# Recurrent mixing and mixture-of-experts layer: another order for the first two turns, 32-byte list entries, logits kept in place, and waits of the scattered adds moved to SyncE

## The reference, cut to what matters

```python
x = x + wkv(w, u, layernorm(x), ctx)        # 16 sequences of 128 tokens, 512 channels
h = layernorm(x)
router = softmax(h @ gate_w.T)              # 8 experts, the best 2 of each token
moe = sum over the 2 of prob * (silu(h @ g_e.T) * (h @ u_e.T)) @ d_e.T      # 256 wide
sh = (silu(h @ sg.T) * (h @ su.T)) @ sd.T   # shared expert, 1024 wide
out = x + moe + sigmoid(h @ seg.T) * sh
```

## Time and profile before

| what | us |
|---|---|
| median of three runs | 589.91 |
| lowest and highest of them | 588.55, 594.93 |
| the profiled execution's own time | 594.29 |
| its span in the trace | 592.4 |
| PE busy in the span | 499.7 (84%) |
| DVE, POOL, ACT busy | 424.5, 334.8, 276.9 |

### The profile page before, as it was taken

The page is one execution under the profiler, slowest core; times in us unless marked ns, Lnnn a source line. Parts: engine busy times, 40 slices in busy tenths (PEclk is TensorE's granted clock), DMA queues, the critical chain, the costliest instruction groups (busy, mean ns, idle before and its releaser), DMA issues.

```text
span 592.4 us, 10167 instructions
## 1 busy us (share of the span) xinstructions
PE 499.7 (84%) x2703; PEld 266.4 (45%) x2703; DVE 424.5 (72%) x986; ACT 276.9 (47%) x534; POOL 334.8 (57%) x421
## 2 busy tenths in 40 slices
PE   1025899899989999999999976899999999999950
PEld 1012355455545555555554543455545555555520
DVE  4398896989888899898998875366656556555530
ACT  4639847484754765847645431333323233323210
POOL 5185956848657478486684450425364655555342
PEclk9999889999989999999999989799999999999995
DMA  8941105224544142132110400315566666766552
GB/s 313 394 172 32 37 18 178 37 71 143 45 82 161 38 148 83 55 143 72 55 35 24 143 18 20 91 35 105 97 109 104 116 108 108 132 111 115 92 71 36
DMA packets 25896, 58.42 MB, mean 99 GB/s; under 512 B 6308, under 2 KB 6450, under 8 KB 24306
## 3 DMA queue, kind: packets, MB, share of 16 engines
q0 software_dynamic: 9792, 20.65, 20.2%
q1 hardware_dynamic: 16050, 37.13, 19.7%
HBM read 37.69 MB, written 20.08 MB: 98 GB/s over the span
## 4 chain that ended last, share of the span: by engine, by line
PE 37%; DMA 17%; issue 13%; DVE 11%; POOL 7%; ACT 7%; POOLq 6%; SPq 1%; DVEq 0%; ACTq 0%
PE GU L878 21%; DMA out<-wall,idsa 11%; PE DN L893 10%; POOLq L575 5%; DMA xb<-x 4%; ACT wall L700 2%; PE HT L823 2%; PE XT L823 2%; DVE st L1076 2%; DMA out<-xb 1%; DVE wall L1066 1%; POOL out L579 1%; DVE hb L1192 1%; DVE th L1189 1%; POOL lists L469 1%
## 5 line engine op out<-in xcount | busy, mean ns | idle before, releaser
L878 PE MATMUL GU<-wall,xt 128*128 128x512 f16 x768 | 192.2, 392 | 4.4 <-DVE wall L1170 4.4
L893 PE MATMUL DN<-wall,hx 128*128 128x512 f16 (+1 forms) x618 | 153.1, 384 | 9.0 <-DVE hx L1197 5.2
L878 PEld LDWEIGHTS GU<-wall,xt 128*128 128x128 f16 x768 | 76.9, 102 | 75.9 <-issue 10.9
L579 POOL DMA_INDIRECT out<-wall,idsa x39 | 61.8, 1585 | 81.5 <-issue 41.5
L893 PEld LDWEIGHTS DN<-wall,hx 128*128 128x128 f16 x618 | 60.4, 99 | 85.3 <-DVE hx L1197 9.4
L657 ACT ACTIVATE hx<-HT 128x256 f16<-128x256 f32 x103 | 39.1, 380 | 125.8 <-PE HT L823 119.7
L1197 DVE TENSOR_TENSOR hx<-HT,hx 128x256 f16<-128x256 f32 x103 | 43.1, 419 | 64.8 <-ACT hx L657 49.5
L652 ACT ACTIVATE th<-GU,scl 128x256 f32<-128x256 f32 x103 | 48.6, 472 | 82.9 <-PE GU L878 80.0
L878 PE MATMUL GU<-wall,kb 128*128 x240 | 61.4, 379 | 0.2 <-DVE kb L1371 0.2
L1189 DVE SCALAR_TENSOR_TENSOR th<-th,GU 128x256 f32<-128x256 f32 x103 | 41.6, 404 | 24.7 <-ACT th L652 21.9
L878 PE MATMUL GU<-wall,xnb 128*128 x228 | 58.5, 379 | 0.2 <-DVE xnb L1371 0.2
(11 more groups left out here) (164 smaller groups left out, 756.4 us busy)
## 6 DMA issues: line engine op xcount, KB each, us to landing
wall<-wgu SPq DMA_DIRECT2D x12, 1024.0 KB, 9.0
wall<-wd SPq DMA_DIRECT2D x12, 512.0 KB, 10.6
xb<-x SPq DMA_DIRECT2D x16, 256.0 KB
cb<-ctx_t SPq DMA_DIRECT2D x16, 256.0 KB
xn_rows<-xnb SPq DMA_DIRECT2D x16, 256.0 KB
out<-xb SPq DMA_DIRECT2D x16, 256.0 KB
out<-yb SPq DMA_DIRECT2D x4, 256.0 KB
xb<-xn_rows,idsi POOLq DMA_INDIRECT x39
```

The lines of the kernel that those rows point to most:

```text
L579: pool.indirect_dma_start(out, bass.IndirectOffsetOnAxis(ap=idsa[:, j:j + 1], axis=0), ye[j % RESULTS], None, compute_op=ALU.add).then_inc ...
L878: ins = nc.tensor.matmul(GU[par][:], lhs(xp, c), gate_up(base, wp, c), start=m == 0, stop=m == 3 * HC - 1)
L893: ins = nc.tensor.matmul(DN[:], hx[par][:, hp * IE + c * P:hp * IE + (c + 1) * P], down(base, wp, c), start=start and m == 0, stop=stop an ...
```

## The change

Seven edits, made together:

1. The lists for tiles 0 and 1 have another order on POOL, ACT, PE and DVE. `keys(0)` goes ahead of the decay terms. The statistics of tile 2 go behind `add_now(1)`. On ACT the squares of a unit are cut in two (`gu_square`, `d_square`) and the exponentials and `second_norm(0)` come between them.
2. Zeros and padding numbers come from the row buffers 3, 4 and 5 of `xb`, not from `yb` and `xnb`. The waits of `quotient(0)` and `second_norm(0)` go, and `load_x(3)` gets one. `load_x(2)` is issued ahead of the eight DMAs.
3. An entry of a list has 32 bytes (LW = 8 int32), so a scatter writes 32 bytes a token and the initial DMA and the gather of the lists move eight times the bytes. `ids_back` lies in the growth and decay buffers, and the copy L1404 takes every eighth element.
4. The logits are written to their final place by ACT, and the maximum by DVE; two copies (L1140, L1141) go, and TOP_STEPS falls from 5 to 3.
5. The waits of the adds stand on SP. SP loads the four numbers, waits, and raises `may_add`; POOL waits for that alone.
6. `shared_gu_lo(1)` stands ahead of the turns instead of in turn 2.
7. `first_stats` waits for the former statistics to have been taken.

```diff
-TOP_STEPS, GATE_STEPS, NORM_STEPS, SCALE_STEPS = 5, 1, 3, 10
+LW = 8
+TOP_STEPS, GATE_STEPS, NORM_STEPS, SCALE_STEPS = 3, 1, 3, 10
...
-        ids_dram = nc.dram_tensor("lists", ((LISTS + 1) * P, 1), I32).ap()
+        ids_dram = nc.dram_tensor("lists", ((LISTS + 1) * P, LW), I32).ap()
...
+        zeros, pad_rows = xb[:, 3 * XW:3 * XW + H], xb[:, 4 * XW:4 * XW + P * LW]
...
             def load_x(t):
+                if t == 3:
+                    sp.wait_ge(ids_zst, ZEROS * 16)
...
+            load_x(2)
             sp.wait_ge(ids_zero, 2)
-            sp.dma_start(xn_dram[PADS:PADS + P, 0:H], yb[:]).then_inc(ids_zst, 16)
+            sp.dma_start(xn_dram[PADS:PADS + P, 0:H], zeros).then_inc(ids_zst, 16)
...
-            load_x(2)
-            sp.dma_start(ids_tiles[0:LISTS, :], xnb[:, 0:P].bitcast(I32)).then_inc(ids_zst, 16)
+            sp.dma_start(ids_tiles[0:LISTS, :], pad_rows.bitcast(I32)).then_inc(ids_zst, 16)
...
+            sp.wait_ge(waits_rdy, WAIT_STEPS)
+            for j in range(1, NSLOT):
+                for r in range(min(j, RESULTS)):
+                    if j < RESULTS:
+                        sp.wait_ge(added[r], 16)
+                    else:
+                        earlier = sp.value_load(before_i[0:1, r * NSLOT + j:r * NSLOT + j + 1],
+                                                min_val=16, max_val=16 * ((NSLOT + RESULTS - 1) // RESULTS))
+                        sp.wait_ge(added[r], earlier)
+                        plain(sp, earlier)
+                sp.sem_inc(may_add, 1)
...
             def quotient(t):
-                if t == 0:
-                    pool.wait_ge(ids_zst, ZEROS * 16)
...
             other_consts()
+            first_product(0)
             norm(1, 0, agg1, norm1, k_rdy)
-            first_product(0)
             second_product(0)
-            pool.wait_ge(nd, 1)
-            norm(2, 0, agg1, norm1, k_rdy)
+            scales(0, ROUTER)
+            nc.gpsimd.tensor_scalar(scale(ROUTER, YINV), scale(ROUTER, TANH), 2.0, None,
+                                    ALU.mult).then_inc(scale_step, 1)
+            quotient(0)
             first_product(1)
             second_product(1)
-            quotient(0)
-            scales(0, ROUTER)
-            nc.gpsimd.tensor_scalar(scale(ROUTER, YINV), scale(ROUTER, TANH), 2.0, None,
-                                    ALU.mult).then_inc(scale_step, 1)
-            pool.wait_ge(nd, 2)
             norm(0, 1, agg2, norm2, xn_rdy)
             scales(1, SHARED)
+            norm(2, 0, agg1, norm1, k_rdy)
+            quotient(1)
             norm(3, 0, agg1, norm1, k_rdy)
-            quotient(1)
             first_product(2)
             second_product(2)
...
                 if j == 0:
                     pool.wait_ge(out_st, 16 * B)
-                if j == RESULTS:
-                    pool.wait_ge(waits_rdy, WAIT_STEPS)
-                for r in range(min(j, RESULTS)):
-                    if j < RESULTS:
-                        pool.wait_ge(added[r], 16)
-                    else:
-                        earlier = pool.value_load(before_i[0:1, r * NSLOT + j:r * NSLOT + j + 1],
-                                                  min_val=16, max_val=16 * ((NSLOT + RESULTS - 1) // RESULTS))
-                        pool.wait_ge(added[r], earlier)
-                        plain(pool, earlier)
+                wait_from(pool, may_add, j)
...
             first_norm(0)
             both_exps(0)
-            shared_square(0)
+            gu_square(0)
             first_norm(1)
-            shared_square(1)
+            d_square(0)
+            gu_square(1)
             both_exps(1)
-            shared_square(2)
-            first_norm(2)
-            shared_square(3)
+            d_square(1)
...
+            gu_square(2)
+            d_square(2)
+            gu_square(3)
             second_norm(0)
+            d_square(3)
             act_hi(0)
             shared_gu_hi(0)
+            first_norm(2)
             shared_gu_hi(1)
...
             keys_t(1)
+            y_back(0)
+            xn_t_(0)
+            sum_squares(1, 2 * SU + 1, 0)
             pe.wait_ge(consts, CONSTS)
             keys_t(2)
-            y_back(0)
-            sum_squares(1, 2 * SU + 1, 0)
-            xn_t_(0)
             y_back(1)
...
+            keys(0)
...
-            keys(0)
             first_stats(1)
             small_steps(k=0)
-            keys(1)
             scan_e(0)
             scan_ev(0)
             add_now(0)
-            first_stats(2)
+            keys(1)
             reciprocals(0, 0, HC)
+            residual_and_stats(0)
             scan_e(1)
             scan_ev(1)
+            small_steps(k=1)
             add_now(1)
-            residual_and_stats(0)
-            small_steps(k=1)
-            first_stats(3)
-            reciprocals(1, 0, HC)
-            keys(2)
+            first_stats(2)
...
             act_lo(0)
+            reciprocals(1, 0, HC)
             shared_gu_lo(0)
+            first_stats(3)
+            keys(2)
+            shared_gu_lo(1)
...
-                if t is not None:
-                    TS(span(lga, t * E, E), lgt[:, 0:E], 1.0, None, ALU.mult).then_inc(top, 1)
-                    TS(span(mxa, t, 1), mx8[:, 0:1], 1.0, None, ALU.mult).then_inc(top, 1)
```

More of the change, by code:

```diff
@@ L137, in build @@
         kb, yb, xnb = sb("kb", [P, H]), sb("yb", [P, H]), sb("xnb", [P, H])
-        growth, decay = sb("growth", [P, HC * T]), sb("decay", [P, HC * T])
+        by_time = sb("by_time", [P, 2 * HC * T])
+        growth, decay = by_time[:, 0:HC * T], by_time[:, HC * T:2 * HC * T]
         th = [sb(f"th{i}", [P, IE]) for i in range(2)]
@@ L382, in other_consts @@
                 assert link.n == CONSTS
-                pool.memset(yb[:], 0.0).then_inc(ids_zero, 1)
-                pool.iota(xnb[:, 0:P].bitcast(I32), [[1, P]], base=PADS, channel_multiplier=0).then_inc(ids_zero, 1)
+                pool.memset(zeros, 0.0).then_inc(ids_zero, 1)
+                pool.iota(pad_rows.bitcast(I32), [[1, P], [0, LW]], base=PADS, channel_multiplier=0).then_inc(ids_zero, 1)
             def norm(t, k, stats_rdy, steps, used):
@@ L614, in second_norm @@
                 wait_from(act, xn_st, 16 * t)
-                if isinstance(t, int) and t == 0:
-                    act.wait_ge(ids_zst, ZEROS * 16)
                 nc.scalar.activation(xnb[:], xrow(t), ACT.Identity, bias=nrm[:, 1, 3:4],
@@ L1304, in logits_off_max @@
                 step(TT(r_d[:, first * E:last * E].rearrange("p (t e) -> p t e", e=E),
-                        lga[:, first * E:last * E].rearrange("p (t e) -> p t e", e=E),
-                        mxa[:, first:last].unsqueeze(2).to_broadcast([P, n, E]), ALU.subtract))
+                        lga[:, first * RN:last * RN].rearrange("p (t e) -> p t e", e=RN)[:, :, 0:E],
+                        mxa[:, first * 8:last * 8].rearrange("p (t e) -> p t e", e=8)[:, :, 0:1].to_broadcast([P, n, E]),
+                        ALU.subtract))
             def probabilities(k, first, last):
```

49 lines of the change are left out of this document (24 added, 25 removed).

## The result

The changed kernel takes 571.84 us (median of 4 runs, 571.03 to 573.75) against 591.96 us for the kernel before in the same comparison (4 runs, 588.55 to 594.93). The ratio is 0.9666, with a 95% interval of 0.9600 to 0.9733: some 20 us faster. The forecast was 566.0, with a range of 556 to 577. So the sign and the range held, and the gain was put some 6 us too high. The profiled execution took 573.75 us, the longest of the four, with a span of 570.1.

What follows compares the result with a forecast made beforehand. The prediction took PE to bound the middle (busy 84% of the span), with gains where it idles or runs slow. Terms 9 + 6.1 + 3.8 + 0 + 4.6 + 4.4 = 27.9 took 594.29 to 566.4; it said 566, range 556 to 577.

Steps and rivals of the forecast that it cites:

- start: First tiles, up to PE's start on the shared units: waits for tile 2's x and the zeros go, 9 us (4 to 12).
- store and load near 160, and passage: 32-byte entries quicken the store and load near 160 (3.8 us) and the passage from turns to slots (6.1 us).
- logits: Turns: two small DVE copies go, gaining 0 (0 to 5), since `chosen` is held in place of L1140.
- slots and tail: Adds with their waits on SP: 4.6 us in the slots (3 to 6), 4.4 at the end (2 to 6).
- the 45 that it had named as a sign of being wrong: Start: the prediction called itself wrong if PE starts on the shared units later than 45 us.
- the reciprocals run about 18 to 21.3: Start, DVE: the reciprocals run there instead of 29.27 to 32.6, 11 us earlier.
- to 29.3; PE's sum and DVE's exponents end near 31, POOL's scales (3 us) near 34: Start: ACT's last weight square ends at 29.3, so ACT makes the first high half at 34 instead of 44.03.
- 34.4 + 3.35 + 2.33 = 40.1 for PE's start: Start: with DVE's `reciprocals(1)` ahead of the low half, PE starts at 40.1 against 49.65.
- The lower end, from the 1664 rows: Scatters of 32 bytes: as quick as the probabilities' 1664 rows of 32 bytes, under 2 ns a row against 31.
- the 3.8 us near 160: Gap and slow products around the slow store and load near 160: 3.8 us gained, perhaps only in the profiled execution.
- no-stall rival: Near 339: `chosen` is not held, or the shifted order misses POOL's subtractions; 561 us, chance 0.12.
- slower rival: Adds: SP's waits exceed PE's 4.58 us a slot, so adds and gathers fall behind; 597 us, chance 0.02.

Runs made afterwards that it cites:

- e2: Changed kernel with list entries still 32 bytes apart, but a scatter writing only the first 4 bytes of each: 571.24 us, ratio 0.9618.
- e3: Changed kernel with the loads and waits of the adds back on POOL instead of SP: 579.99 us, ratio 0.9755.
- f3: Changed kernel with every number of the adds loaded and waited for twice on SP: 624.04 us, ratio 1.0541.
- e4: Changed kernel with entries of 4 bytes and the adds' loads and waits back on POOL: 588.77 us, ratio 0.9909.
- e1: Changed kernel with list entries of 4 bytes again (LW = 1): 581.08 us, ratio 0.9792.
- e5: Changed kernel with POOL's fill of zeros and padding numbers moved behind `second_product(0)`: 571.56 us, ratio 0.9655.
- e6: Changed kernel with the last square of the shared weights ahead of `second_norm(0)` on ACT and its sum ahead of `xn_t_(0)` on PE: 568.09 us, ratio 0.9602.
- e8: Changed kernel with the edits of e5, e6 and e7 together, and `y_back(1)` behind the first unit on PE: 569.17 us, ratio 0.9603.
- e7: Changed kernel with `first_product(2)` ahead of `norm(3, 0)` on POOL: 571.36 us, ratio 0.9664.
- f1: Changed kernel with list entries 16 bytes apart, of which a scatter writes 4 bytes: 568.51 us, one execution.
- f4: Changed kernel with the edits of e6 and e7, and ACT's `shared_gu_hi(3)` moved from ahead of the turns into turn 2: 567.95 us, ratio 0.9599.
- f2: Changed kernel with list entries 8 bytes apart, of which a scatter writes 4 bytes: 572.58 us, one execution.

## Why the prediction was right, and where it was wrong

The sum of the prediction beside the profiled executions:

| term | predicted | by the trace | by the runs |
|---|---|---|---|
| start | 9 (4 to 12) | 3.4 at the store of tile 2 (4.9 to 5.2 in e2, e3, f3) | 3.8 (e4 to before; 3.1 to 7.8) |
| store and load near 160, and passage | 3.8 + 6.1 (0 to 13.5) | 10.5 up to the first add | 9.8 (e1 to e2) |
| logits | 0 (0 to 5) | 0 | not run |
| slots and tail | 4.6 + 4.4 (5 to 12) | 8.4 | 8.8 (e3 to e2) |
| sum | 27.9 | 22.3 | 21.3 (e2 to before) |

**The start: wrong, and this is the step that failed.** The prediction's term of 9 us was 3.4 in the profiled execution, under its own lower bound of 4, and 4.9 to 5.2 in those of e2, e3 and f3, which have the same start (hidden values at 53.2 to 53.6). So it was 4 to 6 us too large. PE's start at 44.80 was all but the 45 that it had named as a sign of being wrong. By its steps:

- "the reciprocals run about 18 to 21.3": they ran from 19.89. `first_stats(1)` came at 13.14, for which x of tile 1 had to land (12.8, e5), and the scans of `scan_e(0)` stand behind it. The list as followed had neither that landing nor the decay operations at 3.41 us, and 1.9 us were missing.
- "`norm(0, 1)` near 27": 30.78. Its three operations took 1.05, 1.38 and 0.27 us beside DVE's scans, where those of the next norm, at 37.91, took 0.22, 0.57 and 0.26, and their statistics came 2.2 us late.
- "to 29.3; PE's sum and DVE's exponents end near 31, POOL's scales (3 us) near 34": the order was seen ("has `second_norm(0)` next and the last square behind it"), but its price was taken for small. Behind the late norm the square ended at 32.6, and the high half came at 37.86. e6 shows that this order alone cost 3.4 us at the high half and 2.7 at the hidden values.
- "34.4 + 3.35 + 2.33 = 40.1 for PE's start": the low half was there at 42.35. And `y_back(1)`, which stands ahead of the first unit on PE, wasn't in the sum at all. It waited for a quotient of 3.24 us on POOL, and PE started at 44.80.
- The last fault is one of kind: PE's start was taken for the milestone that counts. e8 has PE start at 39.81 and gains nothing by it, since the `tanh` behind the first group waits for ACT. The term should have been followed to the hidden values (58.33 before, 53.40 after), and from there to the store of tile 2.

Between those hidden values and the store of tile 2, 4.9 us of gain became 3.4. The products from 72.81 in the kernel after took 2.72 us for six, those of 75.32 1.93 instead of 1.46: the clock fell to half there, behind a wait of PE of 2.2 us, and the products behind it had nothing to wait for. In e2, with the same start, it fell near 67.6, and much of its cost went into a wait of PE that shrank from 2.16 to 0.88 us. The traces of all the runs show the same two cases. From the start of the hidden values to that store it is 30.8 to 31.0 us in e1 to e4, e6, e7, f1, f3 and f4, and 32.5 to 32.6 in the kernel after, e5, e8 and f2 (31.0 before). So 1.7 us hang on where the fall meets PE's work, and the profiled execution of the changed kernel had the bad case. A part of what e6 seems to gain in its trace (4.35 us at the store) is this, and it is why e8's store comes at 83.11, later than e6's, with the hidden values 0.1 us earlier. What sets the place of the fall was not tried.

**The entries: right, with the reason narrowed.** The lower end, from the 1664 rows, gave the right time: the wait in front of L1004 was 2.4 us as forecast, and the gather 3.1 us behind the last scatter. But the row was taken "since it is the same size, direction and memory", and by e2 the size is not what counts. That entries of 32 bytes also lie far enough apart was luck. The rule of the Trainium skill that was weighed against it ("DMA: Bandwidth & Descriptors", section Specifications) would have left this gain out. These runs don't show whether its threshold holds for the rate of long transfers; but e2 wrote 4 bytes a token and kept the gain whole, so here the measurement decides: a cost of neighbours, not of size. The prediction's worry that "entries of neighbouring tokens will lie side by side" did not come true at 32 bytes and hardly at 16 (3.5 us), but does at 8 (10.4).

The thought "if the 3.8 us near 160 is what it had and the others not" was wrong: the stall is in the profiles of before, e1 and e4. It is no mark of one odd execution, and what made the profiled one 4.4 us longer than the median stays open.

**The logits: right.** A `chosen` of 4.22 us stands at 332.10, as forecast, and PE waits behind it. The no-stall rival did not come. Beside it POOL's two subtractions ran from 332.07 for 4.21 us. No run has the edit alone.

**The adds: right.** 8.4 us against 9.0, and in the two parts that were forecast: the last result on DVE stands at 554.82 instead of 572.54, 17.7 us ahead, so 3.8 us came in the slots (4.6 forecast) and 4.6 in the tail (4.4). POOL's slot was put at 4.3 us with the loads and 3.3 without; the adds show 4.2 to 4.3 and 3.19. The last two adds are 2.55 us apart (2.4 forecast), the one of slot 36 is no longer 4.4 us behind its result, and the waits for gathered rows are down to one of 1.2 us. The slower rival did not come, but its price was wrong, as f3 shows: 22 us was worked out for 5.2 us of SP a slot, without the longer steps at the changes of expert, which SP probably hides only while it has a lead.

**The total.** Of the miss of 7.4 us between 566.4 and 573.75, 5.6 us are in the span (27.9 forecast, 22.3 gained), by the table all from the start; 1.8 more is time outside the span, 3.65 us in this execution against 1.9 before.

## What to carry to other kernels

Many small scattered writes into one table were slow when they lay side by side, 4 or 8 bytes apart; before making them larger, space them out (16 bytes were nearly enough here), and look whether other transfers in the same time (here a store of 256 KB) become quick with them. When an order is changed, follow the new list on every engine to the first result that everything later needs, with the durations of packed operations, and ask at each step what stands behind it in its queue: here one square behind one norm was worth more than a wait that had looked larger. Serial waits are best put on an engine with time to spare, but the margin must be counted for a whole step of the loop: at 2.55 us beside a slot of 4.54 they cost nothing that shows, at 5.4 they cost 52 us. And compare two traces at several milestones and over several executions: one fall of the clock moved one milestone by 1.7 us here, half of what the start had gained.

## What the runs showed of the hardware that was not expected

- Indirect writes of 4 bytes to DRAM, 128 a scatter: from the last scatter's issue to the next step it took 14.9 us with the entries side by side, 10.4 at 8 bytes and 3.5 at 16 (one execution each). At 32 bytes it took 3.1 whether 4 or 32 bytes are written, and that time is DVE's, so the landings took no longer. With the entries side by side it took 2.3 to 8.8 us from the issue of a 256 KB store to that of the load behind it (at most 8.8, 8.4 and 8.6 in three traces), where the same eight turns take 2.3 at 32 bytes.
- A small operation of DVE can be held by POOL for far longer than it runs: `chosen`, 128x2, took 4.22 us (median 0.168), and a norm of 128x1 on POOL took 1.05 and 2.18 us beside DVE's scans and low halves (0.22 alone). When the held operation L1140 was removed, its neighbour was held instead.
- A number loaded and waited for once more on SP adds 0.7 us: (5.4 - 2.55) / 4.
- Two executions with the same start to within 0.1 us (hidden values at 53.40 and 53.45) were 1.6 us apart 30 us later, by where the granted clock fell to half (near 72.9 and near 67.6). Over 13 traces of the changed kernel and its variants there are two cases and nothing between: 30.8 to 31.0 us nine times, 32.5 to 32.6 four times.
